# Attention on one core: two key tiles a unit move from the running sum to TensorE's sums, and the sums stand earlier

## The reference

```python
shift1, scale1, shift2, scale2 = split(swiglu(cond @ w_t1 + b_t1) @ w_t2 + b_t2, 4)
h = rmsnorm(x, g1) * (1 + scale1) + shift1
q, k, v = split(h @ w_qkv + b_qkv, 3)          # rope on q and k
p = softmax(q @ k.T / sqrt(32))                # 2048 x 2048 per head
x = x + (p @ v) @ w_ao + b_ao
h = rmsnorm(x, g2) * (1 + scale2) + shift2
x = x + swiglu(h @ w_fc + b_fc) @ w_fo + b_fo
```

## Time and profile before

| | us |
|---|---|
| median of 3 runs | 3174.51 (3170.92 to 3187.06) |
| the profiled execution | 3184.58 |
| its span | 3182.5 |
| PE busy | 3057.4 |
| POOL busy | 1679.6 |
| first unit's first addition starts | 388.6 |
| last unit's first addition starts | 1961.1 |

### The profile page before, as it was taken

One profiled execution on the slowest core, in us unless ns is written; L12 is line 12 of the kernel. 1 busy time (PEld: TensorE's weight loads), 2 busy tenths in 40 slices (PEclk: granted clock), 3 DMA queues, 4 the chain that ended last, 5 costly groups with the idle time before them and its releaser, 6 DMA issues.

```text
span 3182.5 us, 39621 instructions
## 1 busy us (share of the span) xinstructions
PE 3057.4 (96%) x14977; PEld 2050.7 (64%) x14977; DVE 1859.4 (58%) x2970; ACT 1548.0 (49%) x2837; POOL 1679.6 (53%) x718
## 2 busy tenths in 40 slices
PE   7989999999999999999999999799999999999999
PEld 5767655545555555555555554578888888888887
DVE  4668677877878787878878874643333333222222
ACT  4333366766767676767767766432222222111111
POOL 4654578888888888888888888521212200000000
PEclk9999999999999999999999999899999999999999
DMA  6765498898998989989899888532222201121110
GB/s 238 226 180 159 135 194 187 183 198 165 204 191 181 199 182 196 190 179 203 181 199 191 191 198 175 143 112 80 80 80 80 73 20 40 67 84 61 53 53 27
DMA packets 172325, 460.07 MB, mean 145 GB/s; under 512 B 24020, under 2 KB 57896, under 8 KB 140200
## 3 DMA queue, kind: packets, MB, share of 16 engines
q0 software_dynamic: 32256, 234.90, 37.1%
q1 hardware_dynamic: 139352, 221.60, 23.5%
q10 hardware_dynamic: 528, 1.05, 0.1%
HBM read 141.86 MB, written 80.74 MB: 70 GB/s over the span
## 4 chain that ended last, share of the span: by engine, by line
PE 40%; POOL 28%; DMA 20%; issue 8%; DVE 2%; ACT 1%; SPq 0%; POOLq 0%; DVEq 0%; ACTq 0%
POOL b_acc L883 20%; DMA b_pt<-b_pt 19%; PE e_g L1557 11%; PE e_a L1557 11%; PE e_y L1568 10%; POOL b_acc L900 4%; PE e_p L1502 2%; POOL a_q_lo L366 2%; PE a_qk L561 1%; POOL a_yq L359 1%; PE b_s L990 1%; PE b_o L1038 1%; PE a_tv L583 1%; POOL b_pt L906 1%; PE e_y L1502 0%
## 5 line engine op out<-in xcount | busy, mean ns | idle before, releaser
L922 DVE TENSOR_REDUCE b_mpart<-b_m 128x1 f32<-128x512 f32 x1960 | 1200.1, 679 | 331.9 <-PE b_m L974 331.6
L869 ACT ACTIVATE b_pt<-b_s 128x512 f32<-128x512 f32 x2048 | 1089.2, 602 | 427.0 <-PE b_s L990 365.5
L883 POOL TENSOR_TENSOR b_acc<-b_acc,b_pt 128x2048 f32<-128x2048 f32 x224 | 1044.9, 4665 | 227.1 <-DMA b_pt<-b_pt 226.4
L990 PE MATMUL b_s<-b_qs,b_ks 98*128 98x512 f32 x2048 | 859.2, 422 | 52.8 <-ACT b_pt L869 38.9
L974 PE MATMUL b_m<-b_ks,b_qs 96*128 96x512 f32 x1960 | 759.6, 407 | 0.0
L990 PEld LDWEIGHTS b_s<-b_qs,b_ks 98*128 98x128 f32 x2048 | 392.3, 192 | 384.8 <-issue 190.5
L1038 PE MATMUL b_o<-b_pt,b_vg 128*32 128x512 f32 x4096 | 511.0, 618 | 0.1
L974 PEld LDWEIGHTS b_m<-b_ks,b_qs 96*128 96x128 f32 x1960 | 374.8, 191 | 125.6 <-DVE b_mpart L922 55.1
L1437 DVE SCALAR_TENSOR_TENSOR e_u_lo_f<-e_a,keep_chan,e_u_lo_f 128x512 f32<-128x512 f32 x128 | 96.1, 750 | 544.1 <-PE e_a L1557 544.0
L1557 PE MATMUL e_g<-e_h_hi,e_w 128*128 128x512 f32 x1024 | 338.8, 392 | 13.7 <-DVE e_h_lo L1381 8.1
L1557 PE MATMUL e_a<-e_h_hi,e_w 128*128 128x512 f32 x1024 | 338.0, 391 | 0.0
(11 more groups left out here) (144 smaller groups left out, 2959.7 us busy)
## 6 DMA issues: line engine op xcount, KB each, us to landing
b_pt<-b_pt POOLq DMA_DIRECT2D x224, 1024.0 KB, 8.5
scratch_qk_hi<-a_q_hi SPq DMA_DIRECT2D x64, 256.0 KB
scratch_qk_lo<-a_q_lo SPq DMA_DIRECT2D x64, 256.0 KB
b_qs<-scratch_qk_hi SPq DMA_DIRECT2D x64, 256.0 KB, 6.6
b_ks<-scratch_qk_hi SPq DMA_DIRECT2D x28, 512.0 KB, 6.5
scratch_v<-a_vsb SPq DMA_DIRECT2D x32, 256.0 KB, 2.7
b_qs<-scratch_qk_lo SPq DMA_DIRECT2D x32, 256.0 KB, 9.2
b_vg<-scratch_v SPq DMA_DIRECT2D x16, 512.0 KB, 5.6
```

The source lines that it names most:

```text
L869: act.activation(pt[:, kt % RING, h, :], ps_s[:, score_place(i) % LEAD, :], ACT.Exp, scale=SCALE).then_inc(p_ready, 1)
L883: pool.tensor_tensor(acc[u % 2][:], acc[u % 2][:], pt[:, (2 * n + 3) % RING, :, :], ALU.add).then_inc(pool_added, 1)
L922: dve.tensor_reduce(mpart[n % 2][:, i // 4, i % 4:i % 4 + 1], ps_m[:, at, :], AX.X, ALU.max).then_inc(max_done, 1)
L990: pe.matmul(ps_s[:, place % LEAD, :], ks[n // NJ % 2][0:QR, h, kt * P:(kt + 1) * P], qs[n % 4][0:QR, h, :], start=True, stop=True).then_in ...
```

## The change

`PAIRS` goes from 7 to 6: key tiles 14 and 15 are no longer added by transfer and POOL, but stay in the ring (buffers 6 and 7), and `denominators` sums them in the same bank ahead of `acc`, 12 matmuls instead of four. Their buffers are free once these sums are done (`d_ps`). The sums stand behind key tile 4 and no longer behind key tile 7. At the end, one addition instead of two remains for stage e.

```diff
-PAIRS = NK // 2 - 1
+PAIRS = NK // 2 - 2
-SUMS_AT = 4 * 8 + LEAD
+SUMS_AT = 4 * 5 + LEAD
...
-    D_AT = 7
+    D_AT = 4
...
-        return ADDS * u + ADDS + (n + 3 if n < PAIRS - 1 else 2 + ADDS)
+        return ADDS * u + ADDS + (n + 3 if n < PAIRS - 1 else 2 + ADDS - (u == UNITS - 1))
...
         if old < 2:
             eng.wait_ge(pool_added, ADDS * v + ADDS + 1)
+        elif old >= NK - 2:
+            eng.wait_ge(d_ps, v + 3)
         elif old % 2 == 0:
             pair_landed(eng, v, old // 2 - 1)
...
     def gpsimd_late(pool, k):
         if k:
-            pool.sem_inc(pool_added, 1)
-        add_pair(pool, UNITS - 1, PAIRS - 2 + k)
+            add_pair(pool, UNITS - 1, PAIRS - 1)
...
             for n in range(1, PAIRS):
                 fold_pair(u, n)
-                if u < UNITS - 1 or n < PAIRS - 1:
-                    add_pair(pool, u, n - 1)
+                add_pair(pool, u, n - 1)
...
     def denominators(pe, u):
-        pe.wait_ge(pool_added, added(u - 1, PAIRS - 1))
-        for h in range(GH):
-            last = pe.matmul(ps_s[h * HD:(h + 1) * HD, SUMS_AT % LEAD, :], ones[:, 0:HD], acc[(u - 1) % 2][:, h, :], start=True, stop=True)
+        for n in (NK - 2, NK - 1, NK):
+            if n == NK:
+                pe.wait_ge(pool_added, added(u - 1, PAIRS - 1))
+            for h in range(GH):
+                last = pe.matmul(ps_s[h * HD:(h + 1) * HD, SUMS_AT % LEAD, :], ones[:, 0:HD],
+                                 acc[(u - 1) % 2][:, h, :] if n == NK else pt[:, n % RING, h, :], start=n == NK - 2, stop=n == NK)
         last.then_inc(d_ps, 1)
```

## The result

The changed kernel takes 3406.62 us (median of 4 runs, 3405.36 to 3407.81), the kernel before 3173.75 (4 runs, 3170.92 to 3187.06). The ratio is 1.0712, 95% interval 1.068 to 1.0744: the change makes it 233 us slower. The profiled execution took 3407.81, its span 3406.0 against 3182.5.

The account below looks back on a forecast made before the run. It took PE's floor of 48.42 us a unit plus late POOL and transfers as the bound; units 1 to 29 +197.6, units 30 and 31 +13.7, tail +2 gave 3398, less 3: 3395 us, range 3370 to 3420, 8 in 10 3315 to 3450.

Parts of the forecast that it names:

- The floor of 48.42: Attention stage: PE issues without a gap in undisturbed unit 12, which sets a floor of 48.42 us a unit.
- The 50.16 with the eight matmuls: PE's floor a unit once the added matmuls' 1.74 us are counted, about level with today's 50.43 us.
- The eight matmuls: On PE in the sums: two more heads' groups of four a unit cost 1.74 us, bounds 0 and 1.94.
- The wait: PE ahead of the sums: key tile 5's exponential waits for POOL's last addition, 4.65 us in each of 31 units.
- POOL is on time there: At pair 0's transfer: POOL falls back about 1 us a pair over six, then catches up at the unit's turn.
- Rival 4: POOL late at the new place too, last addition 2 to 3 us later in three units of four: 3455 us, chance 0.09.
- The clock: PE after the gap ahead of the sums: low granted clock costs 2.3 us a unit, bounds 0 and 3.0.
- Rival 1: The wait ahead of the sums comes but PE's clock stays up: 54.95 us a unit, 3327 us, chance 0.11.
- 57.25 a unit: Length of an attention unit after the change, in us, with the clock's cost; 54.95 without it.
- Units 30 and 31 and the tail: Last two attention units slow the same way, +13.7 us; end of stage and feed-forward +2, between -5 and +5.
- Rival 2: No wait at key tile 5; PE holds the kernel at 50.16 us a unit: 3176 us, no change, chance 0.04.
- Rival 3: Faster: relief of POOL and DMA removes 2.01 us a unit at key tile 7, matmuls hide: 3126 us, chance 0.04.

Follow-up runs that it names:

- e1: The changed kernel with POOL doing the last addition of the unit before ahead of pair 0's transfer: 3200.65 us, ratio 1.0056 to the kernel before.
- e2: The changed kernel with 19 additional matmuls of a maximum in front of the sums in units 1 to 30: 3339.69 us, ratio 1.0486 to the kernel before.
- e4: The changed kernel with the last addition ahead of pair 0's transfer, and the eight matmuls of key tiles 14 and 15 done twice: 3257.96 us, ratio 1.0227.
- e3: The kernel before with only the sums moved behind key tile 4, still seven pairs and four matmuls: 3408.04 us, ratio 1.0699 to the kernel before.

## Why the prediction was right

Its 3395 was 12 us (0.3%) from the median, inside the likeliest case's own range, and the mechanism is the forecast's.

- The floor of 48.42 from an undisturbed unit: held. Where nothing waits, the steps after are those of before to 0.01 us. The 50.16 with the eight matmuls was 0.25 low against e1's undisturbed units; in the forecast, which takes the second step apart, only 0.12 of it shows (13.32 in e2 for 13.20).
- The eight matmuls, 1.74 us: e4 gives 1.75 by the unit (52.87 - 51.12), 1.85 by the medians.
- The wait. Addition's end at 7.76 after the products, sums at 8.49, wait 4.65: measured 7.67, 8.41 in nearly all units, 8.43 in the mean, so 4.59. It was read off one pair of rows of POOL and the order of its instructions. e1 shows the cause, by removing it. Why PE has to wait there had two reasons, key tile 13's buffer and the sums' own need of the addition; the prediction worked with the first, and e3 shows that the second alone is enough.
- That POOL is on time there: held in 28 of 29 units (pair 0's transfer at 2.25 to 2.27 after the products, once at 3.0). The way to it was off: POOL was to fall back 1 us a pair over six, and pair 5's transfer is issued 4.2 us after its products in the mean, only 2.0 later than an undisturbed one. Rival 4 fell for this kernel and appeared in e3.
- The clock, 2.3 us a unit: 2.29 by e2. Rival 1 fell. That the size fits to 0.01 is luck: 2.3 was a choice between the costs of two waits, 1.7 and 3.0. That every unit pays isn't: the second step after lies between 14.49 and 16.11 where 13.32 is full speed, so the cost is from 1.2 to 2.8.
- 57.25 a unit against 57.74 measured: the missing 0.49 is 0.33 in step 6-7, 0.06 in step 7-0 and 0.11 in the second. Step 6-7 ends in the wait for the next unit's maxima rows (10.1 us of waits of PE's scores for that transfer in units 1 to 29). I had counted it at its undisturbed length, and the 2.01 us a unit above the floor as all POOL's; 0.16 of them were this step's already (6.27 before for 6.11). Over 29 units the 0.49 are 14 us, of which step 6-7 is 10, the largest mis-sized term. It also makes the units less regular than the 55 to 58 forecast: they take 56.3 to 60.3, seven of them over 58.
- Units 30 and 31 and the tail: +13.0 against +15.7. Up to the last products of unit 31 it is +12.4 (forecast +13.7), from there to the end +0.7 (forecast +2). ACT does wait there, as forecast, now with a weight behind it:

```profile
2303.87 1.06 ACT L1273 ACTIVATE e_w<-e_raw 128x1024 fp32r<-128x1024 f32 x1 [6.84 <-PE b_s L959]
```

- The step from 3398 to 3395 wasn't needed: the two profiled executions differ by 223.2 us and the medians by 232.9, since before's profiled execution was 11 us above its median and after's 1 us. Against the profiled execution the sum of +213 was 10 us short; the 14 us of the units are partly made up by the term for units 30, 31 and the tail, which was 2.7 too high, and by a start of unit 1 that came 1.4 earlier.

Rival 2 (level with before) would nearly have come out with POOL's other order: e1, at 3200.65, is 25 us above its 3176. By the unit that is 51.12 for 50.16: the low floor, late additions and the maxima rows. Rival 3 fell with e4, since the matmuls hide nowhere.

## What to carry to other kernels

When work leaves the end of a list, look which item is now the last, who wants it, and when. Here two things wanted it earlier than before: the exponential that writes its ring buffer (the wait in the changed kernel's rows), and the sums, which had moved ahead (enough alone in e3). An addition that had been wanted one pair later became the gate of everything behind it, and what preceded it in its queue, a transfer that waits for the other engine's products, set the time. So price a place in a queue by counting from the event that releases it. And price a long wait on PE with its clock: here that was half as much again (2.29 on 4.59 us). An order that wins in one kernel need not win in its neighbour: the same exchange gave back 206 us with six pairs and cost 100 with seven.

## What the runs showed of the hardware

- In the changed kernel PE's idle ahead of the sums (4.4 us in nearly all units, 4.0 to 5.2 in all) was followed by a stretch at a granted clock of 0.50 (1.2 GHz) in each of units 1 to 31; filling it with matmuls (e2) removed it. In the kernel before 2.51 us had been enough, and another idle of 2.50 us, which ended at 1919.4, was followed by a granted clock of 1.00.
- The addition directly behind pair 0's transfer takes 4.80 to 4.83 us in the changed kernel, where PE is idle for most of it, and 4.90 to 4.93 in the filled units of e2, where PE works through it. Additions away from an issue take 4.58 at the median of either.
- With the DMA share in units 1 to 29 down from 0.90 to 0.70 the adding transfer's median landing goes only from 8.5 to 8.0 us, and its shortest stays at 6.9.
